# When a routed feed-forward kernel issues its scatters: fours at two places of a group, and a pace by finished rows

## What is computed

```
x = x + tanh(g_xattn) * attention(layernorm(x), ctx, ctx, Wq..Wo, mask)
z = layernorm(x)                               # 4096 tokens
scores = z @ gate_w + gate_b
topk_vals, topk_idx = top_k(scores, 2); topk_probs = softmax(topk_vals)
h = relu(einsum('td,edf->etf', z, w1) + b1[:, None, :])
y = einsum('etf,efd->etd', h, w2) + b2[:, None, :]
out = einsum('te,etd->td', combine_w, y)       # combine_w: topk_probs at topk_idx
x = x + tanh(g_ffn) * out
```

## Time and profile before

| what | value |
|---|---|
| runs of the kernel before | 507.41 us median (505.67 to 509.38) |
| profiled execution, its own time | 506.01 us |
| its span on the core | 504.2 us |
| TensorE products busy | 418.4 us (83%) |
| vector / activation / GpSimd busy | 53% / 56% / 54% |
| mean granted clock of TensorE | 0.931 |
| scatters to zs (L959) | 64, busy 63.2 us |
| scatters to res (L970) | 78, busy 75.0 us |

### The profile page before, as it was taken

How to read it: one execution, slowest core, us unless ns; L and a number is a source line. 1 busy time by engine, 2 the same in 40 slices (tenths; PEclk the granted TensorE clock), 3 DMA queues, 4 the chain that set the end, 5 groups by cost and what they waited for, 6 DMA issues and landing times.

```text
span 504.2 us, 12347 instructions
## 1 busy us (share of the span) xinstructions
PE 418.4 (83%) x4299; PEld 333.3 (66%) x4299; DVE 268.6 (53%) x1010; ACT 284.4 (56%) x848; POOL 271.8 (54%) x297
## 2 busy tenths in 40 slices
PE   0779889999899999998988777988589999999900
PEld 0455667667667667576756466977479899999800
DVE  1345667777677676776667553433422333233247
ACT  1277868778787778786856711423133444444334
POOL 8536319059498496793942801864755355554500
PEclk9979999999999999999989956998879999999965
DMA  3999999500000000000010052555538677778278
GB/s 74 240 359 410 412 392 216 104 12 14 23 12 23 25 12 23 13 13 29 8 33 14 33 179 81 175 167 168 173 117 251 197 218 233 239 217 247 90 231 280
DMA packets 48155, 72.55 MB, mean 144 GB/s; under 512 B 8054, under 2 KB 32638, under 8 KB 48094
## 3 DMA queue, kind: packets, MB, share of 16 engines
q1 hardware_dynamic: 43549, 62.32, 40.6%
q0 software_dynamic: 4544, 9.45, 5.3%
HBM read 41.83 MB, written 34.66 MB: 152 GB/s over the span
## 4 chain that ended last, share of the span: by engine, by line
PE 74%; issue 8%; DVE 5%; DMA 4%; ACT 3%; SPq 3%; POOL 1%; another core or an unknown queue 1%; DVEq 0%; POOLq 0%; ACTq 0%
PE S L740 7%; PE T L718 7%; PE O L740 7%; PE U L718 7%; PE S L624 6%; PE O L664 6%; PE O L654 6%; PE T L632 6%; PE S L614 5%; PE U L632 5%; ACT P L819 2%; DMA yg<-res 2%; DVE PT L1074 2%; PE E L673 2%; PE E L688 2%
## 5 line engine op out<-in xcount | busy, mean ns | idle before, releaser
L819 ACT ACTIVATE P<-S,nmax 128x120 f32<-128x120 f32 x512 | 135.2, 420 | 6.9 <-DVE nmax L1068 5.4
L959 POOL DMA_INDIRECT zs<-z,posu x64 | 63.2, 988 | 99.6 <-DVE posu L1147 81.0
L970 POOL DMA_INDIRECT res<-yo,dpos x78 | 75.0, 961 | 64.7 <-DVE yo L1231 56.6
L1068 DVE TENSOR_REDUCE nmax<-S 128x4 f32<-128x480 f32 x128 | 75.1, 649 | 37.4 <-PE S L624 32.3
L826 ACT COPY PT<-U 120x512 f32<-120x512 f32 x64 | 39.6, 619 | 52.9 <-PE U L632 51.7
L856 ACT ACTIVATE H<-T,wbuf 128x256 f32<-128x256 f32 x78 | 32.7, 471 | 62.5 <-PE T L718 45.0
L614 PE MATMUL S<-mb_r,I_r 128*128 128x480 f32 x128 | 65.3, 514 | 2.1 <-ACT P L819 1.9
L856 ACT ACTIVATE H<-U,wbuf 128x256 f32<-128x256 f32 x78 | 32.7, 471 | 51.7 <-PE U L718 37.3
L938 POOL TENSOR_SCALAR Kb<-Kt,hm 128x480 f32<-128x480 f32 x32 | 47.0, 1482 | 18.2 <-ACT Kt L840 18.2
L928 POOL TENSOR_SCALAR z<-X,mv,rstd 128x128 f32<-128x128 f32 x64 | 50.2, 791 | 3.0 <-POOL rstd L923 2.7
L1080 DVE RECIPROCAL orec<-O 128x128 f32<-128x128 f32 x32 | 30.6, 957 | 39.2 <-PE O L664 39.2
(11 more groups left out here) (161 smaller groups left out, 654.0 us busy)
## 6 DMA issues: line engine op xcount, KB each, us to landing
wbuf<-wpk SPq DMA_DIRECT2D x39, 578.0 KB
zs<-zero SPq DMA_DIRECT2D x1, 17952.0 KB, 60.2
zin<-zs SPq DMA_DIRECT2D x39, 132.0 KB
yg<-res SPq DMA_DIRECT2D x16, 256.0 KB, 4.2
wpk<-in_w SPq DMA_DIRECT2D x1, 2048.0 KB, 57.7
wpk<-in_w SPq DMA_DIRECT2D x8, 256.0 KB, 9.3
out<-X SPq DMA_DIRECT2D x16, 128.0 KB, 3.4
ctx_sb<-in_ctx SPq DMA_DIRECT2D x1, 1440.0 KB, 16.8
```

Source lines behind the costliest of these rows:

```text
L819: ins = nc.scalar.activation(P[:, n % 4, j, :], a[:, j * LK:(j + 1) * LK], ACT.Exp, bias=nmax[:, n % 4, j:j + 1])
L959: nc.gpsimd.indirect_dma_start(out=zs, out_offset=bass.IndirectOffsetOnAxis(ap=posu[:, F, k, i:i + 1], axis=0), in_=z2[:, F % 2, i, :], in ...
L970: nc.gpsimd.indirect_dma_start(out=res, out_offset=bass.IndirectOffsetOnAxis(ap=dpos[:, n % NDP, h:h + 1], axis=0), in_=yo[:, n % NYO, h, ...
L1068: v.tensor_reduce(nmax[:, n % 4, :], Sb[n % NHG][:, 0:HG * LK].rearrange("p (j k) -> p j k", j=HG), AX_X, ALU.max, negate=True).then_inc(m ...
```

## The change

The parts of a group are scattered four and four, in p=1 and p=3 two groups later, where before it was two in p=1, two in p=3 and four in p=0 of the third group later. Groups 5 to 7 have places of their own. In rounds 1 to 32 a part waits (`behind_sums`) until TensorE has done the sums of the same round. The last normalising (group 7) moves from round 34 to round 33, and the parts of group 6 stand in rounds 33 to 36, behind it. In the drain every scatter, of the groups 6 and 7 and of results, also waits for a number of finished rows that `paced` gives: the n-th scatter (from 0) waits for 4n // 5 - 1 rows. NYO goes from 6 to 10, and with it NDP from 10 to 14.

```diff
-SCATTERS = {0: (-3, (2, 3)), 1: (-2, (0,)), 2: (-2, ()), 3: (-2, (1,))}
-LAST_SCATTERS = {0: (), 1: (0,), 2: (1, 2), 3: (3,)}
+SCATTERS = {0: (-2, ()), 1: (-2, (0, 1)), 2: (-2, ()), 3: (-2, (2, 3))}
+LAST_SCATTERS = {0: (), 1: (0, 1), 2: (2,), 3: (3,)}
...
-NYO = 6
+NYO = 10
...
+            def behind_sums(k):
+
+                if 1 <= k <= B:
+                    pool.wait_ge(pv_done, k)
+
+            turn = {"next": 0}
+
+            def paced():
+
+                turn["next"] += 1
+                return (turn["next"] - 1) * 4 // 5 - 1
+
             def scatter(F, part, parts):
...
                         if (2 * i + k) * parts // (2 * GB) != part:
                             continue
+                        if F >= SB0[1]:
+                            wait(pool, yo_done, paced())
                         nc.gpsimd.indirect_dma_start(
...
-                pool.wait_ge(yo_done, TH * N0[b] + q + 1)
+                pool.wait_ge(yo_done, max(TH * N0[b] + q + 1, paced()))
...
-                if 0 <= G + F < NG and G + F + 1 not in LAST:
+                if 0 <= G + F < NG and G + F + 1 not in LAST and k <= B:
                     for part in parts:
+                        behind_sums(k)
                         scatter(G + F, part, GB)
-                if p == 2 and 0 <= G - 1 < NG:
+                if p == (2 if G < NG else 1) and 0 <= G - 1 < NG:
                     pool.wait_ge(ln2_step, at(G - 1, 2, 2))
...
                     normalise(z2[:, (G - 1) % 2, :, 0:D], G - 1, mv2, rstd2, z2_done, rstd2_done)
+                if B < k <= B + GB:
+                    scatter(NG - 2, k - B - 1, GB)
                 if G - 1 in LAST:
                     for part in LAST_SCATTERS[p] if G < NG else range(GB) if p == 1 else ():
+                        behind_sums(k)
                         scatter(G - 2, part, GB)
```

## The result

The changed kernel takes 512.43 us (median of 4 runs, 511.96 to 514.38); the kernel before, beside it, 508.39 us (4 runs). The ratio is 1.009, 95% interval 1.0058 to 1.0123: slower by about 1%, where 493.4 us had been forecast and 482 to 510 given. The profiled execution has an own time of 512.86 us and a span of 511.1 us, 6.9 us more than before.

A forecast was written before the change was run, and what follows sets the result against it. TensorE was taken to bound the kernel, through gaps beside GpSimd's scatters. -2.8 + 3.6 + 0.5 - 4.2 - 4.8 - 1.3 + 1.0 - 6.0 = -14.0 us on 506.0 gave 492.0, or 493.4 us at the median; range 482 to 510 us.

The forecast's parts named there:

- The bound and the place of the loss: Whole kernel: TensorE, 74% of the chain, sets the end; GpSimd matters only by the gaps its scatters make on TensorE.
- -2.8 us for the fours of p=0: Attention groups: four bad bunches in p=0 go, saving 0.86 + 0.68 + 0.66 + 0.63 us.
- +3.6 us for eleven new fours at one gap of 0.33 us each: Attention rounds p=1 and p=3, and group 5 once: each new four costs one TensorE gap; bounds 0 and 0.86 us each.
- -4.2, -4.8 and -1.3 us for the bunches at 254 and 281 us: Late attention rounds: two bunches of six broken up save 4.2 and 4.8 us, and 1.3 us of lower clock.
- z2 0.2 us late: Attention groups, behind the longer p=1 bunch: z2 ends 2.53 us later against 2.3 us slack; a gap hides it.
- +0.5 us for group 0: Group 0, whose first scatters are slower: 0.5 us added once for the late z2.
- +1.0 us for z2 of group 6: Late attention rounds: z2 of group 6 comes 2.5 us later with a slack of only 1.5 us, costing 1.0 us.
- -6.0 us in the drain: Expert tiles: half of 12.9 us of stalls and low clock comes back; one stall of two remains.
- The forecast run of 16 to 25 scatters: Start of the drain: GpSimd starts behind the pace, so one unbroken run of that length, then 1.5 us spacing.
- Rival 3: Drain: 1.5 us spacing is itself too dense, +16 us, so 514, or 515 us at the median; chance 0.15.
- gaps past 390 us: Drain: TensorE gaps there, where it had none, would speak against the forecast and show the spacing too dense.
- The rule of the Trainium skill: A DMA never contends with a compute engine; taken alone, gaps are not the scatters' and the sum would be zero.

The follow-up runs named there:

- quiet chip: Chips 13, 12 and 4, where the unedited kernel before took 476 to 477 us; the changed kernel took 481.24 us there, ratio 1.0106.
- stopping chip: Chips 2 and 10, where the unedited kernel before took 508 to 510 us (medians); the changed kernel's 512.43 us is of this kind.
- the twos with spacing: Changed kernel, last normalising back in round 34, scatters of groups 0 to 4 in four twos: 490.63 us, ratio 0.9622; on a quiet chip 477.35 us, ratio 0.9999.

## Why the prediction was wrong

- **The bound and the place of the loss** were right: TensorE sets the end, and its gaps lie beside runs of scatters. The quiet chip shows it most plainly: the kernel before with the same scatters at the same cadence, no gap, and 30.4 us less in its profile (506.01 and 475.60 us).
- **-2.8 us for the fours of p=0**: right, 0.86 us at the first.
- **+3.6 us for eleven new fours at one gap of 0.33 us each: this step failed.** The p=1 four cost 10.35 - 8.06 = 2.3 us in a group, the p=3 four 8.18 - 7.56 = 0.6 us. Over five groups the rounds of p=1 lose 11.8 us and those of p=3 2.4 us (0.4 to 0.9 in four groups, none in the fifth). The four of 281.49 us, charged with one gap too, makes its block 5.1 us for 2.0 and its round (293.03 - 282.66) - (283.24 - 275.01) = 2.1 us longer than before. That is 16.3 us for 3.6. My upper bound of 0.86 us each was itself the cost of a single place, that of p=0. There the values and a part of the sums were over before the stop began, since the four started 3.7 us ahead of the block (127.18 and 130.88 us). The run at 280.90 us, which I had charged with 4.8 us, was the nearer row: its block too began 2.3 us behind the first scatter, and crawled. I counted its six scatters and not where the block lay in them.
- **-4.2, -4.8 and -1.3 us for the bunches at 254 and 281 us**: came in large part. At the p=3 block of group 6 the changed kernel was 259.45 - 247.55 = 11.9 us late. The next two rounds gave back (267.01 - 247.55) - (274.66 - 259.45) = 4.25 us for 4.2, and the stretch behind the last block (313.32 - 283.24) - (318.59 - 293.03) = 4.5 us for 6.1. The loads of the first tiles still run into the lower clock, now from 306.6 us on.
- **z2 0.2 us late**: 0.47 us of waiting on the quiet chip, group after group 32.5 for 32.3 us. Right mechanism, a small size. The +0.5 us for group 0 and the +1.0 us for z2 of group 6 don't show: the first p=1 round is the shortest of the five (10.35 us), and the transpose at 292.15 us starts without a wait.
- **-6.0 us in the drain**: it was +1.7 us. The forecast run of 16 to 25 scatters came as 13, with one stall of 9.2 us. **This step failed too: I let one of the two old stalls stand for the whole backlog behind the early normalising, so the backlog had no price of its own.** I had read stalls of 3 and 5 us in the trace of before, the second of them inside a run of 13 as well. Its chain has a third, which I left out: at 328.33 us vector stands still for 4.79 us, and TensorE for 1.40 us of it, in the run of seven right behind the normalising. The run without the early normalising gives the price, 7 us; what the spacing gave beside it, 6 us, was spent on it. Also unforeseen: the spacing puts the last scatter to `zs` later, on the quiet chip at 349.79 us for 342.78, and TensorE waits 2.6 us for the next tile, which is that chip's whole loss in the drain.
- **Rival 3** had the right side, and nearly the time (515), by another mechanism. Spacing by rows was not too dense: it helped wherever it was tried. Its mark, gaps past 390 us, is there but small (0.67 us at 396.34, 0.49 us at 418.67; in the 2.28 us without a cause at 423.91 us vector waits, TensorE 0.31 us only).
- **The rule of the Trainium skill** (SBUF — State Buffer, Who interferes with whom: a DMA never contends with a compute engine) fits the quiet chips: no gap beside 38 scatters in a row. On the stopping ones it leaves open what holds three engines beside a run of scatters; if the transfers did it, the rule would fail there. Whether the transfers or their issuing do it, no run here shows.

## What to carry to other kernels

Where short indirect scatters share the time with small products, look not at how many stand in a run alone but at what TensorE does 3 to 5 us after the run's first: a cost read at one place of a round isn't the cost at another. Put them in twos with other work between, and don't let a normalising gather a backlog of them: here that took back what the spacing gave. On a stopping chip the twos with spacing gave 3.8%, on a quiet chip nothing, so take the reading of more than one chip before such an order is called tuned; the change studied here is a loss of 1% on both.

## What the runs showed of the hardware that was not expected

- The same kernel takes 508 us on some chips and 476 us on others, steadily: 504.3 to 510.4 us in 13 runs on chip 10, 475.2 to 478.1 us in 9 on chip 12. Of the 30.4 us between the two profiles 12.3 lie ahead of the drain and 17.3 in it, beside and behind runs of scatters.
- On the stopping chips a run of four at 1.26 us, each 0.96 us of GpSimd, makes TensorE stop 3 to 5 us after its first (3.1 us at the four of 281.49 us, 5.3 us at that of 127.18 us), for a few products at a time (0.30 to 0.41 us idle, sometimes 1.0 to 1.1). A run of thirteen held TensorE and vector for 8.4 and 9.3 us and the activation engine for 6.3, until some 2 us after the last scatter; the thirteen from 352.90 us in the kernel before held TensorE for 4.87 us only. At 1.94 us a four leaves 0.33 us of it. Twos in the rounds leave none.
- GpSimd's own scatters keep their 0.96 us in all of this, on both kinds of chip.
